# Six-layer graph network on one core: normalised activations turned by a DMA transpose instead of by TensorE

## What is computed

```
L0: q, k, v = split_heads(h @ Wq + bq), ...(Wk, bk), ...(Wv, bv)            # 12 heads of 32
    scores = where(adj > 0, q @ k.T / sqrt(32) + beta * adj, -9e15)
    out = softmax(scores) @ v
L1: for l in range(2):                                                      # "directed", two layers
        u = (h @ (h @ Wleft.T).T) / temper  on and above the diagonal of adj, with Wright below it
        a = exp(u) * adj;  a = a / (sum(a) + 1e-10)
        h = relu(layer_norm(a @ (h @ Wlin.T + b)))
L2: for l in range(2):
        a = softmax(h @ h.T / sqrt(384)) * adj;  a = a / (sum(a) + 1e-10)
        ctx = (a upper) @ (h @ Wl.T + bl) + diag(a) * (h @ Ws.T + bs) + (a lower) @ (h @ Wr.T + br)
        h = relu(layer_norm(ctx))
L3: a = softmax((q @ k.T) * 384**-0.5 + adj)  per head;  out = (a @ v) @ Wo.T + bo
```

## Time and profile before

| | |
|---|---|
| Median of 3 runs | 3015.51 us (3014.38 to 3015.76) |
| Profiled execution, its own time | 3016.85 us |
| Its span, first to last instruction | 3015.1 us |
| PE busy | 2874.9 us, 95% |
| DVE busy | 2493.4 us, 83% |
| ACT busy | 1769.2 us, 59% |
| POOL busy | 1397.1 us, 46% |
| Granted TensorE clock, mean | 0.99 |

### The profile page before, as it was taken

One profiled execution on the slowest core, in us unless ns is written; L12 is line 12 of the kernel. 1 busy time (PEld: TensorE's weight loads), 2 busy tenths in 40 slices (PEclk: granted clock), 3 DMA queues, 4 the chain that ended last, 5 costly groups with the idle time before them and its releaser, 6 DMA issues.

```text
span 3015.1 us, 88804 instructions
## 1 busy us (share of the span) xinstructions
PE 2874.9 (95%) x34304; PEld 2231.5 (74%) x34304; DVE 2493.4 (83%) x6895; ACT 1769.2 (59%) x6484; POOL 1397.1 (46%) x2313
## 2 busy tenths in 40 slices
PE   0699999999999999999999999999999999999996
PEld 0577777777777777777777777777777777777774
DVE  7478888888888888888888888888888888888874
ACT  3355665566566566566556656656656655665653
POOL 0145445444444544544544445454454454444443
PEclk9799999999999999999999999999999999999997
DMA  6000000000000000000000000000000000000000
GB/s 212 1 2 14 14 8 14 14 8 14 14 12 11 14 12 10 14 14 8 14 14 8 14 14 12 11 14 12 11 14 14 8 14 14 8 14 14 12 7 9
DMA packets 36091, 50.00 MB, mean 17 GB/s; under 512 B 3680, under 2 KB 35552, under 8 KB 35552
## 3 DMA queue, kind: packets, MB, share of 16 engines
q1 hardware_dynamic: 26464, 31.73, 3.4%
q10 hardware_dynamic: 9216, 12.59, 1.1%
HBM read 31.72 MB, written 12.58 MB: 15 GB/s over the span
## 4 chain that ended last, share of the span: by engine, by line
PE 92%; DVE 4%; POOL 1%; DMA 1%; ACT 1%; issue 1%; SPq 0%; POOLq 0%; DVEq 0%
PE bank L827 65%; PE bank L938 8%; PE bank L884 6%; PE bank L851 4%; PE bank L900 3%; PE bank L876 3%; PE bank L929 1%; PE bank L906 1%; PE bank L889 1%; DVE w_lo L647 1%; ACT t L563 1%; DMA t<-in_weights_dram 0%; DMA beta_col<-in_beta_dram 0%; DVE t L639 0%; DVE means L635 0%
## 5 line engine op out<-in xcount | busy, mean ns | idle before, releaser
L827 PE MATMUL bank<-w_hi,ht 128*128 128x384 f16 x3840 | 1032.9, 327 | 1.3 <-DVE t L707 1.3
L827 PE MATMUL bank<-ht,w_hi 128*128 128x128 f16 x9216 | 836.9, 220 | 12.1 <-DVE ht L685 8.2
L827 PE MATMUL bank<-ht,w_lo 128*128 128x128 f16 x4608 | 806.6, 220 | 0.0
L827 PEld LDWEIGHTS bank<-ht,w_hi 128*128 128x128 f16 x9216 | 721.0, 98 | 62.3 <-issue 29.2
L827 PE MATMUL bank<-w_lo,ht 128*128 128x384 f16 x1920 | 627.5, 327 | 0.0
L563 ACT ACTIVATE t<-t,few 128x128 f32<-128x128 f32 x1536 | 596.0, 398 | 0.7 <-DVE few L716 0.6
L827 PEld LDWEIGHTS bank<-w_hi,ht 128*128 128x128 f16 x3840 | 376.6, 98 | 231.3 <-issue 2.6
L449 POOL TENSOR_TENSOR v<-v,row 128x384 f32<-128x384 f32 x256 | 256.8, 1003 | 572.2 <-ACT v L530 572.2
L827 PEld LDWEIGHTS bank<-ht,w_lo 128*128 128x128 f16 x4608 | 454.0, 99 | 0.0
L554 ACT ACTIVATE qk<-bank 128x256 f16<-128x256 f32 x576 | 218.2, 379 | 301.4 <-PE bank L827 301.4
L544 ACT ACTIVATE ht<-bank 128x384 f16<-128x384 f32 x384 | 188.2, 490 | 320.4 <-PE bank L851 318.9
(11 more groups left out here) (108 smaller groups left out, 5384.1 us busy)
## 6 DMA issues: line engine op xcount, KB each, us to landing
x<-in_x_dram SPq DMA_DIRECT2D x64, 192.0 KB, 2.3
out_dram<-h ACTq DMA_DIRECT2D x64, 192.0 KB, 1.9
t<-in_weights_dram SPq DMA_DIRECT2D x19, 576.0 KB, 4.9
adj<-in_adj_dram SPq DMA_DIRECT2D x64, 64.0 KB, 2.2
row<-in_rows_dram SPq DMA_DIRECT2D x1, 3648.0 KB, 11.5
bias_qk<-in_qk_bias_dram SPq DMA_DIRECT2D x1, 3.0 KB, 11.2
beta_col<-in_beta_dram SPq DMA_DIRECT2D x1, 0.5 KB, 11.0
```

What stands on the lines that cost most here:

```text
L827: m = nc.tensor.matmul(out, a, b, start=(first and n == 0), stop=(last and n == 3 * len(left) - 1))
```

## The change

The step `turn` leaves TensorE and PSUM. ScalarE takes the ReLU of `h` as it lies, unturned, and writes the high half into the first 384 columns of `HS`, a view of the space of `qk`; VectorE writes the low half into the next 384 columns. Then one DMA transpose, issued by SyncE, moves the 128 x 768 float16 to `ht` (6 blocks of 128 x 128). The consumers on TensorE wait for that DMA (`turned_in`) instead of for VectorE. The profile counts three float32 transposes on TensorE for each turn before; there are none after. All five engines' lists are written anew. The set-up and the number of streams stay.

```diff
--- before.py
+++ after.py
@@ -106,24 +106,23 @@
 
 
 TURNS = {
...
-    "sync": "2301",
...
+    "sync": "3020132013120312023102313021",
 }
-LATE = {"tensor": [42, 30, 18], "vector": [48, 31, 16],
-        "scalar": [39, 31, 19], "pool": [17, 11, 4], "sync": [1, 0, 0]}
+LATE = {"tensor": [37, 25, 15], "vector": [49, 33, 19],
+        "scalar": [37, 30, 17], "pool": [17, 11, 4], "sync": [6, 4, 2]}
 
 
 def banks_of(name):
-    return {"load": 1, "turn": 1, "proj": 1, "vals": 1, "scores": HPC, "flip": 1, "mix": 1, "back": 1, "project": 1,
+    return {"load": 1, "proj": 1, "vals": 1, "scores": HPC, "flip": 1, "mix": 1, "back": 1, "project": 1,
             "gram": 1, "aturn": 1, "context": 1, "scale": 1}.get(name, 0)
 
 
@@ -192,11 +191,11 @@
     if engine == "pool":
         return (name in ("load", "stats", "vals", "context", "cnorm", "finish") or name == "scores" and layer == GRAPHORMER
                 or name == "aturn" and not directed)
-    return name == "load"
-
-
-
-RELEASE = {"load": "adj_turned", "turn": "turn_lo", "proj": "proj_lo", "vals": "vals_out", "scores": "scored",
+    return name in ("load", "turn")
+
+
+
+RELEASE = {"load": "adj_turned", "proj": "proj_lo", "vals": "vals_out", "scores": "scored",
            "flip": "probs", "mix": "mixed_hi", "scale": "spread", "aturn": "aturn",
            "back": "x_added", "project": "y", "gram": "gram"}
 
@@ -286,6 +285,7 @@
         RB = [h[:, 0].rearrange("p (h k) -> p h k", h=H) for h in HN]
         OS = [v[:, 0].rearrange("p (c k) -> p c k", c=C) for v in V]
         SUMS = [h[:, 0, 0:H * P // 8].rearrange("p (h k) -> p h k", h=H) for h in HN]
+        HS = [q[:, 0].rearrange("p c a t -> p (c a t)") for q in QK]
         SQUARED = [q[:, 0].rearrange("p c a t -> p (c a t)")[:, 0:D] for q in QK]
         OH = [[q[:, half, :, 0, :] for half in range(2)] for q in QK]
         B0 = [p[:, 0:G] for p in PT]
@@ -323,6 +323,7 @@
         done = [{name: sem(f"{name}{s}") for name in plan.total} for s in range(STREAMS)]
         filled = [sem(f"bank_filled{s}") for s in range(STREAMS)]
         x_in = [sem(f"x_in{s}") for s in range(STREAMS)]
+        turned_in = [sem(f"turned_in{s}") for s in range(STREAMS)]
         stored = [sem(f"stored{s}") for s in range(STREAMS)]
         w_in = [sem(f"w_in{i}") for i in range(4)]
         w_centred, w_hi_done, w_lo_done = sem("w_centred"), sem("w_hi_done"), sem("w_lo_done")
@@ -350,9 +351,20 @@
 
             eng.wait_ge(done[s][sig], count(r, plan.total[sig], plan.nth[sig, step][n]))
 
+        def wait_for_normed(eng, r, s, layer, i):
+
+            if layer in (DIR_B, DIG_B):
+                wait_for(eng, r, s, "biased", ("cnorm", layer - 1, i))
+            else:
+                wait_for(eng, r, s, "normed", ("norm", layer, i))
+
         def wait_for_vals(eng, r, s, layer, i):
 
             wait_for(eng, r, s, "valued" if (layer, i) in VALS_ON_VECTOR else "biased", ("vals", layer, i))
+
+        def wait_turned(eng, r, s, layer):
+
+            eng.wait_ge(turned_in[s], 16 * (6 * nth_round(r) + layer + 1))
 
         def wait_filled(eng, r, s, step, j=0):
 
@@ -415,6 +427,9 @@
                     n = nth_round(r) * STREAMS + s
                     sp.dma_start(X[s][:], x_v[bass.ds(n, 1)].rearrange("a p g d -> (a p) g d")).then_inc(x_in[s], 16)
                     sp.dma_start(A[s][:], adj_v[bass.ds(n, 1)].rearrange("a p g d -> (a p) g d")).then_inc(x_in[s], 16)
+                elif name == "turn":
+                    wait_for(sp, r, s, "turn_lo", step)
+                    sp.dma_start_transpose(HT[s][:].rearrange("p w c t -> p (w c) t"), HS[s]).then_inc(turned_in[s], 16)
 
             rounds(sp, "sync", step_of)
 
@@ -540,10 +555,8 @@
                                          accum_out=SS[s][:, i:i + 1]).then_inc(done[s]["squares"], 1)
                 elif name == "turn":
 
-                    wait_filled(act, r, s, step)
-                    nc.scalar.activation(HT[s][:, 0, :, i * P:(i + 1) * P],
-                                         bank_of(s, step)[:, 0:D].rearrange("p (c k) -> p c k", c=C),
-                                         ACT.Relu).then_inc(done[s]["turn_hi"], 1)
+                    wait_for_normed(act, r, s, layer, i)
+                    nc.scalar.activation(HS[s][:, 0:D], HN[s][:, i], ACT.Relu).then_inc(done[s]["turn_hi"], 1)
                 elif name == "proj":
                     wait_filled(act, r, s, step)
                     if layer == GAT:
@@ -682,10 +695,8 @@
                                             ALU.mult).then_inc(done[s]["normed"], 1)
                 elif name == "turn":
                     wait_for(v, r, s, "turn_hi", step)
-                    nc.vector.scalar_tensor_tensor(
-                        out=HT[s][:, 1, :, i * P:(i + 1) * P], in0=bank_of(s, step)[:, 0:D].rearrange("p (c k) -> p c k", c=C),
-                        scalar=0.0, in1=HT[s][:, 0, :, i * P:(i + 1) * P], op0=ALU.max,
-                        op1=ALU.subtract).then_inc(done[s]["turn_lo"], 1)
+                    nc.vector.scalar_tensor_tensor(out=HS[s][:, D:2 * D], in0=HN[s][:, i], scalar=0.0, in1=HS[s][:, 0:D],
+                                                   op0=ALU.max, op1=ALU.subtract).then_inc(done[s]["turn_lo"], 1)
                 elif name == "proj":
                     wait_for(v, r, s, "proj_hi", step)
                     if layer == GAT:
@@ -842,18 +853,9 @@
                     for g in range(G):
                         last = nc.tensor.transpose(bank_of(s, step)[:, g * P:(g + 1) * P], A[s][:, g], ident)
                     last.then_inc(filled[s], 1)
-                elif name == "turn":
-                    if layer in (DIR_B, DIG_B):
-                        wait_for(pe, r, s, "biased", ("cnorm", layer - 1, i))
-                    else:
-                        wait_for(pe, r, s, "normed", ("norm", layer, i))
-                    for c in range(C):
-                        last = nc.tensor.transpose(bank_of(s, step)[:, c * P:(c + 1) * P], HN[s][:, i, c * P:(c + 1) * P],
-                                                   ident)
-                    last.then_inc(filled[s], 1)
                 elif name == "proj":
 
-                    wait_for(pe, r, s, "turn_lo", ("turn", layer, G - 1))
+                    wait_turned(pe, r, s, layer)
                     for side in range(2):
                         last = product(bank_of(s, step)[:, side * TOK:(side + 1) * TOK],
                                        [weight(W0[layer] + side, c, slice(i * P, (i + 1) * P)) for c in range(C)],
@@ -862,7 +864,7 @@
                 elif name == "vals":
 
                     j, g = i // G, i % G
-                    wait_for(pe, r, s, "turn_lo", ("turn", layer, g))
+                    wait_turned(pe, r, s, layer)
                     product(bank_of(s, step)[:, 0:D], [turned(s, c, slice(g * P, (g + 1) * P)) for c in range(C)],
                             [weight(W_V[layer][j], c) for c in range(C)]).then_inc(filled[s], 1)
                 elif name == "scores":
```

19 lines of the change are left out of this document (9 added, 10 removed).

## The result

| | time, median | range | ratio to before, 95% interval |
|---|---|---|---|
| before | 3015.64 us (4 runs) | 3014.38 to 3015.92 | |
| after | 3118.03 us (4 runs) | 3117.22 to 3121.92 | 1.0343 [1.0325, 1.0361] |

The change costs 102 us, 3.4%. The forecast was 2945 us. The profiled execution of the kernel after took 3121.92 us, 3.9 over its median.

A forecast was written before the change was run, and what follows sets the result against it. TensorE was taken as the bound, so whatever leaves its stream shortens the kernel. 3016.85 - 127 + 32 (DMA) + 10 (VectorE) + 15 (ends) = 2946.9, less 1.3 for the median: 2945 us, range 2885 to 3115.

The forecast's parts named there:

- What leaves TensorE: TensorE's stream: 1152 transposes go, 0.33 us for each of 384 turns, saving 127 us, 7.9 of a round's 178.4.
- What ScalarE and VectorE do instead: Turn halves read from SBUF, not PSUM: under 1 us a round on ScalarE, 559 ns against 556 on VectorE; no cost.
- The DMA: From VectorE's end to TensorE's start: 3.0 us, 0.5 over the room at layer 3's `gram`, 64 times, 32 us.
- Rivals 1 and 2: First: DMA hidden altogether, landing within 2.5 us, TensorE never waits, 2915 us, chance 0.22. Second: see rival 2.
- SyncE's queue: SyncE's list of transposes: 24 in a 170.5 us round leave 7.1 us for each; nothing counted.
- Rival 3: DMA ring is the bound if a transpose holds its queue over 7.1 us; at 8 us, 3260 us; chance 0.08.
- VectorE's new wait: Layer 2's turn directly behind scaling of the same `h`: VectorE stands still 7.2 us a round; 10 us allowed per run.
- Rival 4: VectorE becomes the bound, half its old waits staying beside the new: round 174.5 us, about 2970 us, chance 0.08.
- The ends: First and last graphs: turns 2.4 us longer, six make 14 us at each end, about half covered: 15 us.
- What would show it: Signs in the profile after: two rounds 341 to 345 us if right, 357 or more in rival 2; landing near 3 us.
- rival 2: TensorE waits at `gram` and `proj` longer than saved: slower beyond a 4.1 us DMA, 3120 at 4.9 us; chance 0.22.
- the forecast's 2915 without the DMA term: Whole kernel: forecast base in us with the 32 us of TensorE's waits for the DMA left out.

The follow-up runs named there:

- no_dma: Changed kernel without its DMA transposes; SyncE raises the same semaphore at once after VectorE's half, all orders kept: 3103.91 us, 1.0292 of before.
- bare: Changed kernel, own order, without DMA transposes and with GpSimd's three bias additions cut to one column of 384: 3008.18 us, 0.9974 of before.
- replanned_b: Changed kernel with other hand-written orders on all five engines, same DMA transpose per turn, more steps between loads or stores and their readers: 3021.74 us, 1.0019 of before.

## Why the prediction was wrong, point by point

- **What leaves TensorE, 127 us.** The 0.33 us a turn stand in the trace (8.0 us a round from start to start, 7.9 counted), but the gain was taken one to one. By itself, in the old order, TensorE's time brought 44 for 84 us. "TensorE is the bound there, and whatever leaves its stream shortens the kernel" was true for about half the way.
- **What ScalarE and VectorE do instead, nothing.** L698 takes 574 ns where L685 took 556, 7 us in all. The kind was right, the condition was missed: the instruction now has two inputs in SBUF and can meet GpSimd, as at 1167.07 us (0.69 us, inside L473).
- **The DMA, 3.0 us and 32 us of waits.** It lands in 2.7 us, near the 2.8 that the prediction had worked out from the Trainium skill, "DMA: Bandwidth & Descriptors", section "Latency and other measured facts". TensorE waited 62.5 us for it, in 64 places, but only 14 of them make the run longer (no_dma). Rivals 1 and 2 both fall: the DMA is not wholly hidden, and it is far from 4.1 us.
- **SyncE's queue, nothing.** Right: 1.21 us a transpose of the 7.7 that each has. Rival 3 falls.
- **VectorE's new wait, 10 us in the whole run.** This is the step that failed. The wait was read correctly out of the order, 7.2 us a round and 6.7 measured. But it was set against VectorE's total ("159.5 of 170.5, so VectorE still has 11 us"). An engine need not be full to make the round: 11.4 us of its list stand in series with 34.5 us of TensorE's, and only 8.1 us of TensorE's work lie beside them. The chain of after does not run over the wait, and bare shows that the series sets the round. Its price, with the meetings in it, is the 13.8 us a round.
- **Rival 4** saw VectorE as the rival and gave 2970, by busy time and old waits again. It foretold VectorE over 90% busy; it is 83% (85% of the steady stretch), and still the kernel is slower.
- **The ends, 15 us.** 12 us measured.
- **What would show it.** The distance of the nine adjacency transposes, forecast at 341 to 345 us and at 357 or more for rival 2, is 368.5; but it was no sign of rival 2, since the DMA is the least of TensorE's waits.
- **What the prediction did not have at all:** the additions on GpSimd that block VectorE, 82 us. L810 at 559 ns is nearly free of them, because the old order kept the two apart. One of its 128 instances did say what a meeting costs: it took 1329 ns.

The sum with measured terms: the forecast's 2915 without the DMA term, + 93 (what bare keeps: the order, and whatever else came with the change) + 82 (GpSimd's additions) + 14 (the DMA) + 14 (both together) = 3118. Of the mechanism itself only the 14 are certain to belong to it; the meetings and the 93 depend on the order, and replanned_b shows that an order takes 96 us of the 102 back. The kernel before was not run with its additions cut, so that the 82 us are new is read from L821 and L676 alone. What is not settled is whether an order exists in which the DMA version is faster than 3015 us; none of those tried was.

## What to carry to other kernels

Before pricing what leaves a full engine, follow the new order's longest series that crosses engines: TensorE's part of the loop plus the other engine's part, against the engine's total. A removed load is worth its time only up to the next loop, and one experiment that removes the load and nothing else shows where that is. And when a fixed order is changed, every pair of instructions that were kept apart, here GpSimd's additions and VectorE's readers of SBUF, must be looked for again: two moved steps were worth 54 us of 3118.

## What the runs showed of the hardware

- A VectorE instruction with two SBUF inputs (L821, 128x384 float32) takes 1.35 us when it starts inside a GpSimd addition of the same size, and 0.55 alone; a `tensor_scalar` on 128x128 (L676) 0.83 us and 0.22. It is blocked and then runs at full length: 1169.03 - 0.55 = 1168.48, 0.14 us before the end of the addition. L676 says the same: beside L464 it ends 0.08 to 0.09 us behind the addition, whether it started 0.24 us into it (0.83 us long) or 0.72 us (0.36 us long, one case). The other way round too: L521 takes 1.31 us in place of 0.99, as it began inside L698. The Trainium skill, "SBUF — State Buffer", section "Who interferes with whom", has the rule: a VectorE instruction with two SBUF inputs contends with a GpSimd instruction that reads SBUF, the pair of ports is locked and not shared, and the order of issue decides who blocks. It names `tensor_scalar` among the operations that can take both ports. The trace agrees: L821 and L698, with two SBUF inputs, and L676 are the ones that wait, the wait ends close to the end of the other's instruction, and either engine can be the one that waits.
- A DMA transpose from SBUF to SBUF of 128x768 float16 lands 2.7 us after its issue and holds SyncE 1.21 us; one of 128x384 lands after 2.4 us and holds it 1.18. The Trainium skill, "VectorE: DVE Perf Modes", section "The three transpose paths", gives 1309 ns by DMA for one block of 128 x 128; six blocks did not take six times that here, so the prediction was right not to build its sum on that rule.
- TensorE busy for 1796.8 of 1800 us did not mean that its stream was the only bound: 84 us less of it brought 44.
